# Causal attention with its heads side by side in 64-row tiles of float32r instead of three bfloat16 parts

## The chip, the cores and the metric

The kernel runs on one core of a Trainium2 chip. The time is device microseconds from launch to end, as the median of several runs. The core has five engines that run side by side: TensorE (matrix products, results into the eight banks of PSUM), VectorE, ScalarE, GpSimd and SyncE, whose queue SP starts transfers.

## What is computed

One layer on x of shape (2, 1024, 128), in float32: a modulated layer norm, causal attention with 16 heads of 8 numbers each, a residual, a second modulated norm and a mixture of eight experts (two for each token) with a shared one. Only the attention is changed. Cut to it:

```python
c_q = x @ W_dq
Q = (c_q @ W_uq).reshape(Bx, Sx, N_HEADS, D_K)
c_kv = x @ W_dkv
K = (c_kv @ W_uk).reshape(Bx, Sx, N_HEADS, D_K)
V = (c_kv @ W_uv).reshape(Bx, Sx, N_HEADS, D_K)
scores = jnp.einsum('bqhd,bkhd->bhqk', Q, K) / math.sqrt(D_K)
causal = jnp.tril(jnp.ones((Sx, Sx), dtype=bool))
scores = jnp.where(causal, scores, -jnp.inf)
attn = jax.nn.softmax(scores, axis=-1)
out = jnp.einsum('bhqk,bkhd->bqhd', attn, V).reshape(Bx, Sx, N_HEADS * D_K)
return out @ W_o
```

D_K is 8, Sx is 1024, and there are two batches.

## The kernel before

**Tasks.** The attention is cut into eight tasks, four heads of one batch each, and every task into two halves c of 512 queries. A task goes through two passes. In the first, `max_scores` (L1685) multiplies 128 queries by up to 512 keys for one head, and VectorE reduces each such unit to the row maximum (`max_unit`): a plain reduction (L1286) where all keys are allowed, and on the diagonal a combined add of a mask `later` and maximum (L1282). `maxima` (L1295) joins them, GpSimd splits the negated maxima into three bfloat16 parts (`split_max`, L674 to L677), TensorE turns them (`turn_max`, L1694), VectorE copies them (`neg_out`, L1303), and SP writes them as three more rows of the operands (`neg_rows`). In the second pass `score_unit` (L1716) multiplies 128 keys by up to 512 queries, so that the product comes with its maximum already subtracted. On the diagonal a product of the identity and the mask `after` is added (L1721). ScalarE takes the exponential (`exps`, L941). `weigh` (L1740) multiplies by the values, four heads at once in four 32-column tiles, in float32, and adds up in the bank `oacc[:, c]`; each of its products appears as two records in the trace. ScalarE copies that bank (`o_out`, L950), TensorE transposes it (`turn_out`, L1749), and VectorE divides (L1318, L1320).

**Operands.** A float32 number is the sum of three bfloat16 parts, made by `hi`, `residue`, `mid` and `low`. The parts go to memory and come back replicated, so that one contraction over 9 x 8 = 72 rows (CROSS) holds all products of parts; three rows of ones, or of the maxima, make 75. They lie in `S3`, a ring of three tasks, with a K side and a Q side. `load` brings one task: `load_k` three transfers, `load_q` three for each half.

**Order.** `attention_order` writes one list for all engines, and each engine walks through it in that order. The maxima run ahead of the scores: AHEAD units first, then some after every score unit (MAXES_AFTER), about a task of lead. The turn of the maxima stands SPLIT units behind their last one. A group (128 keys of one half) is weighed LAG score units after its last one; in all but the first and last task two groups are weighed together. BETWEEN and LATE put the late projections, the second norm and the router in between. FILLERS and FILL_AFTER are products without use early in the first task (`fill`).

**PSUM.** Three banks `sc` for scores, three `mx` for maxima and other units (`unit_banks` hands them out in turn), two `oacc`. `ring_free` makes TensorE wait until the engine that read a bank's last unit has freed it. So a score unit waits for the exponential three units back, and a unit of maxima for the reduction three units back.

After the attention come the routed experts: 39 tiles of 128 rows, products of 128 columns in float32 (L1873 and L1888) with the shared expert (L1829, L1840) in between.

## Time and profile before

| what | value |
|---|---|
| median of 3 runs | 430.55 us (429.49 to 431.08) |
| span of the profiled execution | 455.7 us; no other time of it is given |
| TensorE busy | 422.1 us (93%) |
| VectorE busy | 319.5 us (70%) |
| ScalarE busy | 268.1 us (59%) |
| GpSimd busy | 150.0 us (33%) |
| mean granted TensorE clock | 0.949 of full speed |
| first maxima of the attention | 24.1 us |
| first product of the routed experts | about 310 us |

The profile is of one execution. PE is TensorE's products, PEld its weight loads, DVE VectorE, ACT ScalarE, POOL GpSimd. Products are pipelined: one of 512 columns is shown 0.38 us long, while the next may begin 0.22 us after it began, so that distances between starts say more than lengths. The granted clock is 1.00 at 2.4 GHz and 0.50 at 1.2 GHz.

### The profile page before, as it was taken

Reading aid. Unit: us, or ns where it says so; the run is one execution under the profiler, and the core shown is the slowest. Engines: PE = TensorE matmul, PEld = TensorE weight load, DVE = VectorE, ACT = ScalarE, POOL = GpSimd, SP = SyncE. Lnnn points to the kernel's source line nnn. Section 1 sums busy time; section 2 is a strip of 40 time slices with the busy share of each in tenths; the row PEclk is TensorE's granted clock in tenths of the full one; section 3 lists DMA queues with packets and bytes.
Section 4 is the critical chain, followed back from the end, with each engine's and each line's share of the span. In section 5 each row is a group of like instructions: output and inputs, shape, how many; then the busy total and the mean of one; then the engine's idle time right before and its main releaser. Section 6 shows DMA issues by size and latency. Waiting matters only on the chain.

```text
span 455.7 us, 9455 instructions
## 1 busy us (share of the span) xinstructions
PE 422.1 (93%) x2963; PEld 242.9 (53%) x2963; DVE 319.5 (70%) x1185; ACT 268.1 (59%) x611; POOL 150.0 (33%) x244
## 2 busy tenths in 40 slices
PE   6989899999999999999999999999959779999984
PEld 3434423353443544454544434337747569999944
DVE  5768855788887987889797886355866435555646
ACT  3557344556666767675666576967446254555661
POOL 2246200026010020106556434231664743333520
PEclk9998855999999999999999999999989959999999
DMA  5245160034040210400400000960112223210126
GB/s 146 65 141 124 34 192 3 1 101 146 1 106 2 58 51 0 106 3 0 108 7 19 21 21 23 315 149 13 43 46 54 76 65 83 60 40 26 36 85 216
DMA packets 28796, 31.78 MB, mean 70 GB/s; under 512 B 4827, under 2 KB 23363, under 8 KB 28243
## 3 DMA queue, kind: packets, MB, share of 16 engines
q1 hardware_dynamic: 25959, 25.82, 20.0%
q0 software_dynamic: 2272, 4.67, 3.0%
q10 hardware_dynamic: 516, 0.69, 0.5%
q8 instruction: 24, 0.39, 0.4%
q14 instruction: 25, 0.20, 0.2%
HBM read 21.04 MB, written 9.85 MB: 68 GB/s over the span
## 4 chain that ended last, share of the span: by engine, by line
PE 71%; DVE 13%; issue 4%; DMA 4%; ACT 2%; another core or an unknown queue 2%; POOL 1%; SPq 1%; ACTq 0%; DVEq 0%; POOLq 0%
PE oacc L1740 15%; PE mx L1685 12%; PE sc L1716 12%; PE sc L1873 7%; PE oacc L1888 7%; DVE mxp L1286 4%; DVE masked L1282 3%; PE sc L1721 2%; PE mx L1840 2%; PE mx L1829 2%; PE mx L1749 1%; PE mx L1864 1%; PE sc L1829 1%; DMA S<-first_q_parts 1%
## 5 line engine op out<-in xcount | busy, mean ns | idle before, releaser
L941 ACT ACTIVATE pr<-sc 128x512 f32<-128x512 f32 (+1 forms) x295 | 156.2, 580 | 93.0 <-PE sc L1716 45.3
L1282 DVE CUSTOM_DVE_ANT_0 masked<-mx,later 128x128 f32<-128x128 f32 (+3 forms) x256 | 111.5, 485 | 19.4 <-PE mx L1685 18.7
L1685 PE MATMUL mx<-S 72*128 72x512 bf16 (+3 forms) x384 | 116.0, 344 | 6.4 <-DVE mxp L1282 2.2
L1716 PE MATMUL sc<-S 75*128 75x512 bf16 (+3 forms) x371 | 112.6, 339 | 0.7 <-ACT pr L941 0.6
L1286 DVE TENSOR_REDUCE mxp<-mx 128x1 f32<-128x512 f32 x128 | 82.9, 685 | 23.5 <-PE mx L1685 23.1
L1740 PE MATMUL oacc<-pr,vb 128*32 128x512 f32 (+3 forms) x768 | 77.9, 515 | 0.0
L1011 ACT ACTIVATE pr<-sc,bcur 128x128 f32<-128x128 f32 x156 | 44.5, 369 | 33.4 <-PE sc L1873 18.4
L1716 PEld LDWEIGHTS sc<-S 75*128 75x128 bf16 x371 | 35.3, 100 | 51.2 <-issue 28.6
L1685 PEld LDWEIGHTS mx<-S 72*128 72x128 bf16 x384 | 35.0, 101 | 48.0 <-DVE mxp L1282 19.2
L783 POOL DMA_INDIRECT token_results<-S,xrow x39 | 38.5, 988 | 61.7 <-DVE S L1432 59.6
L1888 PE MATMUL oacc<-vb,pr 128*128 128x128 f32 x312 | 42.8, 283 | 5.2 <-ACT pr L1011 5.2
L1888 PEld LDWEIGHTS oacc<-vb,pr 128*128 128x128 f32 x312 | 40.6, 199 | 12.8 <-ACT pr L1011 6.8
L1873 PE MATMUL sc<-xTg,vb 128*128 128x128 f32 x312 | 43.5, 284 | 3.5 <-ACT xTg L1003 1.2
L674 POOL CAST neg<-negm 128x16 bf16<-128x16 f32 x16 | 3.1, 196 | 129.2 <-DVE negm L1295 129.1
L1873 PEld LDWEIGHTS sc<-xTg,vb 128*128 128x128 f32 x312 | 39.5, 199 | 4.6 <-issue 3.2
L1721 PE MATMUL sc<-after,identb 128*128 128x128 bf16 (+2 forms) x171 | 41.9, 245 | 0.0
L777 POOL DMA_INDIRECT slot_rows<-parts,rowi x32 | 31.7, 989 | 29.9 <-PE sc L1716 12.1
L1740 PEld LDWEIGHTS oacc<-pr,vb 128*32 128x32 f32 x768 | 19.3, 111 | 35.7 <-issue 17.0
L1432 DVE TENSOR_TENSOR S<-oacc,be_sb 128x128 f32<-128x128 f32 x39 | 11.3, 290 | 31.5 <-PE oacc L1888 20.0
L1417 DVE COPY vb<-S 128x512 f32 x39 | 17.6, 451 | 19.9 <-issue 15.8
L1003 ACT ACTIVATE xTg<-mx 128x128 f32<-128x128 f32 x39 | 11.0, 283 | 22.2 <-PE mx L1864 15.6
L1282 DVE DVE_READ_ACCUMULATOR2_ANT mxp<- 128x1 f32 x256 | 21.0, 82 | 0.0
(294 smaller groups left out, 499.1 us busy)
## 6 DMA issues: line engine op xcount, KB each, us to landing
S<-k_parts SPq DMA_DIRECT2D x21, 192.0 KB
S<-q_parts SPq DMA_DIRECT2D x42, 96.0 KB
xrow<-slot_rows SPq DMA_DIRECT2D x39, 64.5 KB, 1.9
S<-in_we SPq DMA_DIRECT2D x1, 2048.0 KB, 9.7
S<-in_we SPq DMA_DIRECT2D x4, 512.0 KB, 10.4
parts<-token_results SPq DMA_DIRECT2D x4, 512.0 KB, 5.2
x_sb<-in_x SPq DMA_DIRECT2D x4, 256.0 KB, 3.9
out_y<-attn SPq DMA_DIRECT2D x4, 256.0 KB, 2.3
```

The lines of the kernel that those rows point to most:

```text
L777: pool.indirect_dma_start(xd, bass.IndirectOffsetOnAxis(ap=rowi[:, g, k, n:n + 1], axis=0), rowsk[:, g % 2, n, k, :], None).then_inc(sent[ ...
L783: pool.indirect_dma_start(yd, bass.IndirectOffsetOnAxis(ap=xrow[:, i % XR, C:C + 1].bitcast(I32), axis=0), yst[:, i % ROWS, :], None).then ...
L941: act.activation(pr[:, group % NBUF, h:h + n, at:at + w], src, ACT.Exp, scale=float(DK) ** -0.5).then_inc(s["exp_done"], 1)
L1011: ins = act.activation(hid[:, i % 2, P * f:P * f + P], sc[:, i % 2, P * f:P * f + P], ACT.Silu, bias=bcur[:, i % FREE, f:f + 1])
L1282: ins = dve.tensor_tensor_reduce(masked[:, d % 2, w * m:w * m + w], unit[a][:, w * m:w * m + w], later[:, HALF - w:HALF], 1.0, LOWEST, ALU ...
L1286: ins = dve.tensor_reduce(mxp[:, c, place, h:h + n, i - 4 * c], unit[a][:, 0:n * w].rearrange("p (h n) -> p h n", h=n), AX_X, ALU.max)
L1685: ins = pe.matmul(dst[:, w * m:w * m + w], S3[0:CROSS, r3, 1, q:q + P], S3[0:CROSS, r3, 0, kk:kk + w], start=(m == 0), stop=True, skip_gro ...
L1716: ins = pe.matmul(dst[:, w * m:w * m + w], S3[0:CROSS + 3, r3, 0, kk:kk + P], S3[0:CROSS + 3, r3, 1, q:q + w], start=(m == 0), stop=True, ...
L1721: ins = pe.matmul(dst[:, 0:n * w].rearrange("p (h n) -> p h n", h=n)[:, :, 0:P], identb[:, :], after[:, 0:n, :], start=False, stop=True, s ...
L1740: ins = pe.matmul(oacc[VW * h:VW * h + VW, c, at:HALF], vb[:, t % 2, j, h, :], pr[:, group % NBUF, h, at:HALF], start=(j == 0), stop=(j == ...
L1873: ins = pe.matmul(sc[:, i % 2, P * f:P * f + P], wcur[:, i % 2, P * f:P * f + P], xTg[:, i % 2, :], start=True, stop=True)
L1888: ins = pe.matmul(oacc[:, i % 2, 0:P], hid[:, i % 2, P * f:P * f + P], wcur[:, i % 2, FF + C * f:FF + C * f + C], start=(f == 0), stop=(f ...
```

## The change

- *Operands.* K and Q are split in two float32r parts, high and low, made by one ScalarE copy and one subtraction. The contraction has 2 x 2 x 8 = 32 rows, a row of ones or zeros (33 rows for the maxima) and two more for the two parts of the negated maximum (35 for the scores). `mid` and `residue` fall away.
- *Tiles.* Heads 0 and 1 of a task lie in partitions 0 to 63 (side 0), heads 2 and 3 in 64 to 127 (side 1). Each product uses one 64-row tile. A unit of maxima has both sides, in two neighbouring banks; a unit of scores has one side. There are 20 units of maxima for a task (38 before) and 40 of scores (38).
- *Masks.* Both passes add the mask by products over 64 rows, in two parts of 64 columns a head: `rows_of` picks rows, `stairs` holds the lowest number on one side of a diagonal. `later`, `masked` and the combined operation on VectorE are gone; `max_unit` is one reduction over two banks.
- *PSUM.* Four banks for maxima (two pairs), three for scores, one for the weighed sums, which both halves now share, so `weigh` waits at each first group for the copy of the half before.
- *Order.* AHEAD 12, one unit of maxima after each of the first 16 score units, then after every second one. SPLIT is 2. ScalarE copies the turned maxima (it was VectorE). The products without use are three after each of the first eleven units of maxima.
- *Transfers.* A task's operands come in 8 transfers (9 before), the maxima go back in two (one before).

```diff
+F32R = mybir.dt.float32r
...
-CROSS = 72
+PAIR = 2
+SIDE = 64
+PRODUCTS = 32
+ONES_AT = PRODUCTS + 1
 HALF = 512
-QW = HQ * HALF
+QW = PAIR * HALF
...
-            n = HALF // w if w < 384 else 1
+            n = 2 if w <= 256 else 1
             if c:
-                out += [(c, i, h, 1, 0, HALF, False, 0) for h in range(HQ)]
-            out += [(c, i, h, n, HALF * c, w, True, c) for h in range(0, HQ, n)]
+                out += [(c, i, h, 1, 0, HALF, False, 0) for h in range(PAIR)]
+            out += [(c, i, h, n, HALF * c, w, True, c) for h in range(0, PAIR, n)]
...
+            out += [(c, j, side, h, n, q0, w, P * j == q0) for h in range(0, PAIR, n) for side in range(2)]
...
-AHEAD = 20
-MAXES_AFTER = [2] * 4 + [3] * 4 + [2] * 2 + [1] * 5 + [2 if g % 4 == 0 else 1 for g in range(28)]
-FILL_AFTER = {9: 1, 10: 2}
-FILLERS = {(0, k): 2 if k < 3 else 1 for k in (0, 1, 2, 3, 4, 5, 7, 8, 10)}
-SPLIT = 5
+AHEAD = 12
+EXTRA_MAXES = 8
+FILLERS = 3
+SPLIT = 2
...
+          *[("turn", t, c) for t in range(8) for c in range(2)]}
...
+MX, SC, OA = (0, 1, 2, 3), (4, 5, 6), 7
...
+        if g % 2 == 0 or g < 2 * EXTRA_MAXES:
...
+        elif kind == "max":
+            banks = min((MX[0:2], MX[2:4]), key=lambda b: max(used[k] for k in b))
+        elif kind == "xturn":
+            banks = (SC[x[1] % 2],)
+        elif wide:
+            banks = (min((*SC, MX[0]) if kind == "score" else MX[1:4], key=lambda b: used[b]),)
+        elif kind == "score" or x in ON_ACT:
+            banks = (min(SC, key=lambda b: used[b]),)
...
-        sc = ctx.enter_context(nc.psum_tensor("sc", [P, RING, 512], F32))
-        mx = ctx.enter_context(nc.psum_tensor("mx", [P, RING, 512], F32))
-        oacc = ctx.enter_context(nc.psum_tensor("oacc", [P, 2, 512], F32))
+        mx = ctx.enter_context(nc.psum_tensor("mx", [P, 4, 512], F32))
+        sc = ctx.enter_context(nc.psum_tensor("sc", [P, 3, 512], F32))
+        oacc = ctx.enter_context(nc.psum_tensor("oacc", [P, 1, 512], F32))
...
-        after = sb("after", [P, HQ, P], BF16)
-        later = sb("later", [P, HALF], F32)
-        masked = sb("masked", [P, 2, HALF], F32)
+        warmb = sb("warmb", [P, HALF], BF16)
+        stairs = sb("stairs", [P, 2, SIDE], BF16)
+        rows_of = sb("rows_of", [P, 2, 2, P], BF16)
...
-        parts = sb("parts", [P, 2, 3, NT * P], BF16)
+        parts = sb("parts", [P, 2, 2, NT * P], F32)
...
+        with nc.sbuf_tensor("operands", [P, 3, 2, 2 * QW], F32) as S3:
+            S3r = S3[:, :, :, :].bitcast(F32R)
...
-                for a in range(3):
-                    sp.dma_start(S3[24 * a:24 * a + 24, r3, 0, :].rearrange("r (h n) -> r h n", h=HQ)[:, :, cols],
-                                 src).then_inc(sem, 16)
+                for side in range(2):
+                    src = kd[b, u, :, :, PAIR * side:PAIR * side + PAIR, cols].rearrange("d a h n -> (d a) h n")
+                    for a in range(2):
+                        at = SIDE * side + 2 * DK * a
+                        sp.dma_start(S3[at:at + 2 * DK, r3, 0, :].rearrange("r (h n) -> r h n", h=PAIR)[:, :, cols],
+                                     src).then_inc(sem, 16)
...
+            chained(pool.memset(stairs[:, :, :], LOWEST))
+            chained(pool.memset(rows_of[:, :, :, :], 0.0))
+            for side in range(2):
+                half, first = slice(SIDE * side, SIDE * side + SIDE), slice(SIDE * side, SIDE * side + 1)
+                chained(pool.affine_select(out=stairs[half, 0], in_=stairs[half, 0], compare_op=ALU.is_ge, fill=0.0,
+                                           base=0, pattern=[[1, SIDE]], channel_multiplier=-1))
...
-                chained(pool.tensor_copy(neg3[:, c, 0, :], negm[:, c, :]))
-                chained(pool.tensor_tensor(negr[:, c, :], negm[:, c, :], neg3[:, c, 0, :], ALU.subtract))
-                chained(pool.tensor_copy(neg3[:, c, 1, :], negr[:, c, :]))
-                pool.tensor_tensor(neg3[:, c, 2, :], negr[:, c, :], neg3[:, c, 1, :],
-                                   ALU.subtract).then_inc(s["neg3_ready"], 1)
+                chained(pool.tensor_copy(neg2[:, c, :, 0, :].bitcast(F32R), sides(negm[:, c, :])))
+                pool.tensor_tensor(neg2[:, c, :, 1, :].bitcast(F32R), sides(negm[:, c, :]), neg2[:, c, :, 0, :],
+                                   ALU.subtract).then_inc(s["neg2_ready"], 1)
...
+            def neg_out(t, c, a):
+
+                act.wait_ge(s["aux_ready"], a + 1)
+                if t >= 1:
+                    act.wait_ge(s["negrow"], 32 * (2 * t + c - 1))
+                act.activation(negT[:, c, :], unit[a][0:2 * HQ * 4, 0:P], ACT.Copy).then_inc(s["act_free"], 1)
...
+                own = mx[:, HELD["max", t, k][0]:HELD["max", t, k][0] + 2, 0:n * w]
                 dve.wait_ge(s["aux_ready"], a + 1)
-                if diagonal:
-
-                    d = DIAGONAL.index((t, k))
-                    if d >= 2:
-                        dve.wait_ge(*freed(("max", *DIAGONAL[d - 2])))
-                    for m in range(n):
-                        ins = dve.tensor_tensor_reduce(
-                            masked[:, d % 2, w * m:w * m + w], unit[a][:, w * m:w * m + w], later[:, HALF - w:HALF],
-                            1.0, LOWEST, ALU.add, ALU.max, mxp[:, c, place, h + m, i - 4 * c:i - 4 * c + 1])
-                else:
-                    ins = dve.tensor_reduce(mxp[:, c, place, h:h + n, i - 4 * c], unit[a][:, 0:n * w].rearrange(
-                        "p (h n) -> p h n", h=n), AX_X, ALU.max)
-                ins.then_inc(s["aux_free"], 1)
+                dve.tensor_reduce(sides(mxp[:, c, place, :, i - 4 * c])[:, :, h:h + n],
+                                  own.rearrange("p s (m w) -> p s m w", m=n), AX_X, ALU.max).then_inc(s["aux_free"], 1)
 
             def maxima(t, c):
...
+            def operand(r3, side, rows, kq, at, n):
+
+                return S3r[SIDE * side:SIDE * side + rows, r3, kq, at:at + n]
...
-                dst = unit[a]
+                    pe.wait_ge(s[f"first_in{c}"], 16 * 6)
                 for m in range(n):
-                    q = QW * (i // 4) + HALF * (h0 + m) + P * (i % 4)
-                    kk = S * (h0 + m) + k0
-                    ins = pe.matmul(dst[:, w * m:w * m + w], S3[0:CROSS, r3, 1, q:q + P],
-                                    S3[0:CROSS, r3, 0, kk:kk + w], start=(m == 0), stop=True,
-                                    skip_group_check=(m > 0))
+                    q = QW * (i // 4) + HALF * (h + m) + P * (i % 4)
+                    kk = S * (h + m) + k0
+                    for side in (1, 0):
+                        dst = bank[HELD["max", t, k][side]]
+                        ins = pe.matmul(dst[:, w * m:w * m + w], operand(r3, side, ONES_AT, 1, q, P),
+                                        operand(r3, side, ONES_AT, 0, kk, w), start=(m == 0), stop=True,
+                                        skip_group_check=(m > 0))
+                if diagonal:
+                    for part in range(2):
+                        for side in (1, 0):
+                            dst = bank[HELD["max", t, k][side]][:, 0:n * w].rearrange("p (m w) -> p m w", m=n)
+                            at = w - P + SIDE * part
+                            own = slice(SIDE * side, SIDE * side + SIDE)
+                            ins = pe.matmul(dst[:, :, at:at + SIDE], rows_of[own, 0, part, :], stairs[own, 0:1, :].broadcast_to([SIDE, n, SIDE]),
+                                            start=False, stop=True, skip_group_check=True)
...
+                dst = bank[HELD["score", t, k][0]]
                 for m in range(n):
-                    kk = S * (h0 + m) + P * j
-                    q = QW * c + HALF * (h0 + m) + q0 - HALF * c
-                    ins = pe.matmul(dst[:, w * m:w * m + w], S3[0:CROSS + 3, r3, 0, kk:kk + P],
-                                    S3[0:CROSS + 3, r3, 1, q:q + w], start=(m == 0), stop=True,
+                    kk = S * (h + m) + P * j
+                    q = QW * c + HALF * (h + m) + q0 - HALF * c
+                    ins = pe.matmul(dst[:, w * m:w * m + w], operand(r3, side, ONES_AT + 2, 0, kk, P),
+                                    operand(r3, side, ONES_AT + 2, 1, q, w), start=(m == 0), stop=True,
                                     skip_group_check=(m > 0))
                 if diagonal:
-
-                    ins = pe.matmul(dst[:, 0:n * w].rearrange("p (h n) -> p h n", h=n)[:, :, 0:P], identb[:, :],
-                                    after[:, 0:n, :], start=False, stop=True, skip_group_check=True)
+                    own = slice(SIDE * side, SIDE * side + SIDE)
+                    for part in range(2):
+                        ins = pe.matmul(dst[:, 0:n * w].rearrange("p (m w) -> p m w", m=n)[:, :, SIDE * part:SIDE * part + SIDE],
+                                        rows_of[own, 1, part, :], stairs[own, 1:2, :].broadcast_to([SIDE, n, SIDE]), start=False, stop=True,
+                                        skip_group_check=True)
                 ins.then_inc(s["score_ready"], 1)
...
-                if j == 0 and t >= 1:
-                    pe.wait_ge(s["o_done"], 2 * t + c - 1)
-                elif j == 0 and c == 1:
-                    pe.wait_ge(*freed(("val", 3, 0)))
-                if k == 0 and t in BACK:
-                    pe.wait_ge(*freed(BACK[t]))
+                if j == 0 and 2 * t + c:
+                    pe.wait_ge(s["o_done"], 2 * t + c)
                 for h in range(HQ):
-                    ins = pe.matmul(oacc[VW * h:VW * h + VW, c, at:HALF], vb[:, t % 2, j, h, :],
+                    ins = pe.matmul(oacc[VW * h:VW * h + VW, 0, at:HALF], vb[:, t % 2, j, h, :],
...
-                    pe.matmul(dst, identb[:, :], parts[:, 0, 0, 0:HALF], start=True, stop=True)
+                    pe.matmul(bank[OA], identb[0:SIDE, :], warmb[0:SIDE, :], start=True, stop=True)
```

The helpers `freed`, `bank_free` and `unit_banks` are otherwise adapted to the new names: a bank's next user waits for the reader of its last one.

## Rows read from the trace of the kernel before

**Rows 1.** The page: span, busy time of each engine, granted TensorE clock in 40 slices.

```profile
span 455.7 us, 9455 instructions
...
PE 422.1 (93%) x2963; PEld 242.9 (53%) x2963; DVE 319.5 (70%) x1185; ACT 268.1 (59%) x611; POOL 150.0 (33%) x244
...
PEclk9998855999999999999999999999989959999999
```

**Rows 2.** The page: the chain that ended last, by engine and by line.

```profile
PE 71%; DVE 13%; issue 4%; DMA 4%; ACT 2%; another core or an unknown queue 2%; POOL 1%; SPq 1%; ACTq 0%; DVEq 0%; POOLq 0%
PE oacc L1740 15%; PE mx L1685 12%; PE sc L1716 12%; PE sc L1873 7%; PE oacc L1888 7%; DVE mxp L1286 4%; DVE masked L1282 3%; PE sc L1721 2%; PE mx L1840 2%; PE mx L1829 2%; PE mx L1749 1%; PE mx L1864 1%; PE sc L1829 1%; DMA S<-first_q_parts 1%
```

**Rows 3.** The chain in order of time: start us, length us, what.

```profile
105.90 1.89 DVE mxp L1286 x3
110.10 1.85 PE oacc L1740 x16
...
121.73 1.64 PE oacc L1740 x16
125.07 0.79 PE oacc L1740 x16
...
135.44 1.89 DVE mxp L1286 x3
...
165.86 1.89 DVE mxp L1286 x3
...
284.25 0.06 PE sc L1721
...
292.41 1.00 PE oacc L1740 x8
...
378.11 0.89 PE sc L1873 x8
```

**Rows 4.** Windows: busy us of each engine (count), granted clock, DMA share, GB/s.

```profile
52.00:56.00 4.00, 2.96 (x15) 1.46 (x16) 3.52 (x21) 0.88 (x3) 0.97 (x4) 0.77 0.04 9
56.00:80.00 24.00, 24.00 (x90) 6.96 (x92) 13.58 (x41) 9.74 (x17) 0.83 (x4) 0.50 0.33 98
130.00:160.00 30.00, 29.70 (x232) 13.25 (x230) 25.38 (x90) 20.95 (x41) 2.19 (x10) 1.00 0.17 44
```

**Rows 5.** Timeline of TensorE in one steady task: start us, length us, instructions.

```profile
133.21 0.40 PE L1685 MATMUL mx<-S 72*128 72x128 bf16 x4
...
135.02 0.38 PE L1685 MATMUL mx<-S 72*128 72x512 bf16 x1
135.24 0.38 PE L1716 MATMUL sc<-S 75*128 75x512 bf16 x1
...
136.36 0.66 PE L1749 MATMUL mx<-ident,osb 128*128 128x128 f32 x4
```

**Rows 6.** Timeline of VectorE in the same task.

```profile
139.10 1.88 DVE L1286 TENSOR_REDUCE mxp<-mx 128x1 f32<-128x512 f32 x3
...
143.15 0.55 DVE L1282 CUSTOM_DVE_ANT_0 masked<-mx,later 128x384 f32<-128x384 f32 x1
...
143.62 0.55 DVE L1282 CUSTOM_DVE_ANT_0 masked<-mx,later 128x384 f32<-128x384 f32 x1
```

**Rows 7.** Timeline of ScalarE in the same task.

```profile
136.19 3.64 ACT L941 ACTIVATE pr<-sc 128x512 f32<-128x512 f32 x7
```

**Rows 8.** The page: costliest groups, busy us, mean ns, idle us before and its releaser.

```profile
L941 ACT ACTIVATE pr<-sc 128x512 f32<-128x512 f32 (+1 forms) x295 | 156.2, 580 | 93.0 <-PE sc L1716 45.3
...
L1716 PEld LDWEIGHTS sc<-S 75*128 75x128 bf16 x371 | 35.3, 100 | 51.2 <-issue 28.6
...
L1873 PEld LDWEIGHTS sc<-xTg,vb 128*128 128x128 f32 x312 | 39.5, 199 | 4.6 <-issue 3.2
...
L1003 ACT ACTIVATE xTg<-mx 128x128 f32<-128x128 f32 x39 | 11.0, 283 | 22.2 <-PE mx L1864 15.6
```

385 lines of the change are left out of this document (166 added, 219 removed).

## The prediction

> **What bounds it now.** I read the page first: TensorE is busy 93% of the span, and the row of granted clock is full except in a few slices [rows 1]. The chain that ended last is 71% TensorE, led by the weighing of values (L1740) and the two kinds of score products (L1685, L1716); the reductions on VectorE hold 6.5% of it [rows 2]. So the attention is a TensorE stage with VectorE close behind. The windows say how close: in 30 us of steady attention TensorE is busy 29.7, VectorE 25.4, ScalarE 21.0 [rows 4].
>
> The period of a task (four heads of one batch) is read in the chain from a piece that recurs: 105.90, 135.44, 165.86, so 29.5 and 30.4 us; I use 30.0 [rows 3]. There are eight tasks. Their maxima run a task ahead, so the first stretch has many maxima and the last task none.
>
> **TensorE's sum for one task now.** Products: 4,608 columns a head for the maxima and as many for the scores, times four heads, 36,864 columns. Starts of neighbouring 512-column products lie 0.22 us apart (135.02, 135.24) [rows 5]; 72 blocks' worth make 15.7. Masks: 32 blocks of 128 columns at 0.06 us, 1.9 [rows 3]. Weighing: six pairs of groups, 1.64 + 0.79 + 1.85 + 1.85 + 1.64 + 0.79 = 8.6 [rows 3]. Two sets of output transposes, 0.6 each, and two turns of maxima: 1.6. Together 27.8; the other 2.2 are gaps and waits.
>
> **The change on TensorE.** (a) *Products.* A head contracts 33 or 35 rows of float32r instead of 72 or 75 of bfloat16, in a 64-row tile; two heads, one in each half of the rows, write to different banks. The order makes the neighbours alternate: score of side 0, maxima of side 1 and side 0, score of side 1. Columns and count (96 a task) stay. Nothing in this trace shows a row tile or a float32r product, so I bound both. Tiles do overlap on this array: eight weighing records of 512 columns in four column tiles take 1.0 us (292.41) [rows 3], where a float32 record alone takes two cycles a column, 0.11 us for 128 (378.11, eight in 0.89) [rows 3], thus 0.43 for 512 and 3.4 for eight. Below, then: one cycle a column, sides fully overlapped, 7.9 us. There each instruction has only 0.11 us for a 512-column product, and its weights must be loaded in that time. The bfloat16 weight load is 100 ns and streams at 0.055 us each (four products of 128 columns in 0.40, the last's latency taken off) [rows 5, 8]; a float32 load is 199 ns and streams at 0.11 [rows 3, 8]. If that holds here, 96 x 0.111 = 10.7. I take the middle, 9.3. Above, two cycles a column or no overlap give 15.7, and that is a rival below.
>
> The Trainium skill (TensorE: Matmul & The Clock Gate, Weight-path perf modes) says that fast weight load needs a dtype other than FP32. The trace agrees in direction, 199 ns against 100; by the page the sum would be the 10.7 rather than 9.3.
>
> (b) *Masks.* TensorE now masks the maxima as well. A task has 24 diagonal score units and 12 diagonal maxima units of two sides, each with two 64-column products: 96 instead of 22 instructions, for half the rows. At 0.06 each 5.8; if 64 columns or a pair of sides halve that, 2.9; I take 4.3, which is 2.4 more than now. The Trainium skill (TensorEngine Tiling (Array Packing), Instruction Overhead) gives some 60 cycles to any small matmul; by it 64 columns gain next to nothing over 60, and 96 would be an estimated 2.4 to 4.8 us. No row here shows a 64-column product.
>
> (c) *The rest stays*: weighing, transposes, turns, gaps. The alternation of tile shapes before and after each weighing is there now too. Sum: 9.3 + 4.3 + 8.6 + 1.6 + 2.2 = 26.0, bounds 23.2 and 28.9 (7.9 + 2.9, and 10.7 + 5.8).
>
> **What is late next.** *VectorE.* Now the reductions of 512 columns start 0.60 us apart (three in 1.88, the last 0.69 long) and the masked ones of 384 0.48 [rows 6], that is columns / 0.96 GHz plus 0.06 to 0.08: 16 x 0.60 + 8 x (0.21 + 0.35 + 0.48 + 0.61) = 22.8 a task. After: 20 reductions over two banks, the same 18,432 columns / 0.96 = 19.2, plus 20 x 0.065 = 20.5. The other 2.6 us (25.4 - 22.8) lose two copies of the turned maxima, 0.4. So 22.7 a task: the accumulator reads are gone, but VectorE gains only 2.7 of 25.4. *ScalarE.* Exponentials of 512 columns run at 0.51 us (seven in 3.64) [rows 7], 427 ns of columns and 80 fixed; two more units and two copies of about 0.28 (that of 128 columns, L1003) [rows 8] make 21.0 + 0.7 = 21.7. Both lie under 26.0, but three engines within 4 us, with two pairs of banks for the maxima (before, three single ones) and a weighing of 1.85 us blocking TensorE at a time, can't all be fed. Below 24.5 I don't believe it. Taken: 26.2.
>
> *The single output bank.* The next half's weighing waits for ScalarE's copy. It lies four to eight units later, 2 to 4 us against a 0.6 us exponential and a 0.6 us copy; with that cover gone each of 16 handovers would cost up to 0.6. I take 2 us in all. *The turn* comes two units after its last maximum, about 2.5 us, and waits for 0.19 on VectorE and two GpSimd steps (four before) of 0.2; it costs at most some tenths, and queued behind it are the products that both other engines wait for. It is in the 0.2 between 26.0 and 26.2. *Transfers.* A task's operands came in 9 DMAs, 72 rows of 4,096 two-byte numbers a side; now they come in 8, 64 rows of 2,048 four-byte ones, with a task of slack (share 0.17 in the window) [rows 4]. The maxima rows go back in two DMAs instead of one, 40 units before the scores need them. SP's queue before the first stores gets three more, at a time when it waits for the parts. *The start.* A middle part vanishes (two 0.6 us copies, two or three slow GpSimd subtractions), but four instead of three loads follow for each half; I leave it at nothing. GpSimd builds stairs and row patches with some 20 short chained steps, hidden behind the same loads.
>
> **The sum.** Six ordinary tasks save 30.0 - 26.2 = 3.8 each: 22.8. The first, filled by VectorE, saves 2.3 (22.8 - 20.5). The last has no maxima, ScalarE and dependent steps set it: 1 taken. Minus 2 for the bank: 24 us. The profiled execution is known by its span, 455.7, which is 25.1 over the median of 430.55; no other time of it is given. Some of the excess is in places that the change doesn't touch: the 24 us at half clock (12 lost) [rows 4] and waits in the experts. So I take the difference at face value: 430.5 - 24 = 407. Its bounds: 1.1 (28.9) to 5.5 (24.5) in each of six tasks, 7 to 36 in all with the rest, so 395 to 423.
>
> **Rivals.** *1. The products don't get cheaper* (slower). One cause: float32r needs two cycles a column, like each float32 record; or one: the row tiles run one after the other. Either gives 15.7 + 4.3 for 17.6, +2.4 a task (0.9 to 4.0), and eight tasks 19: 450 (437 to 462). It decides as soon as products plus masks exceed 17.6. For it: every one-pass float32 row, the transposes of 128 columns (four in 0.66) [rows 5], starts 0.11 apart, two cycles a column. Against: those may be held by their own weight loads. 19%. Both causes at once, 31.4: 18 us a task, about 575; 4%.
>
> *2. The clock.* At 52 to 56 TensorE was busy 2.96 of 4 us and the clock fell to half; it stayed there until 80 though the engine was busy all 24.0 of the 24 us [rows 4]. After the change TensorE waits more. A task at half clock is 50 us instead of 26, so one task's work in that state takes the whole gain, and two give 455 (430 to 500). Against: 100 to 310 ran at full clock with the present mix, and 26 of 26.2 us is no idle engine. 14%.
>
> *3. The gain is eaten by waits* among VectorE, ScalarE and the pairs of banks: 29 to 30 us a task, 425 to 433. For it: ScalarE already waits 93 us ahead of its exponentials [rows 8]. 11%.
>
> **Numbers.** The forecast has 52%; its time is 407, its own range 395 to 423. About 0.5% (2.2 us) can be told from no change. Faster: 52 + 5 of rival 3 + 1 of rival 2, 58%. Same: 7%. Slower: 35%. The range 395 to 456 holds most of the forecast, rival 3 and the lower part of rivals 1 and 2, some 80%.
>
> **What will show it.** The L1685 and L1716 groups: starts of two sides nearly together and a 512-column pair each 0.22 us (right), or 0.43 (rival 1). The period of a task 26 us; VectorE's reductions of 1,024 columns 1.13 us apart and its busy share near 87%; masks 0.03 to 0.06 each; the clock row full between 100 and 280. Wrong if the weight loads of float32r are longer than 0.11, if small masks drain the array, or if half-clock stretches return.

## The result and the profile after

The changed kernel takes 534.91 us (median of 4 runs, 531.37 to 554.35), the kernel before 430.81 beside it: a ratio of 1.237, 95% interval 1.228 to 1.247. The forecast was 407, its range ended at 456. Executions of one program differ in the clock that they are granted, so the ratios here are of the faster ones alone, and the profile of the kernel before (455.7 us, mean granted clock 0.949, 44 us at half) is of a slower one than its timed runs near 430 us (0.995, by which I estimate some 4 us at half). The page of the changed kernel, in the parts that answer to [rows 1, 2, 8]:

```profile
span 529.9 us, 10032 instructions
PE 496.1 (94%) x3573; PEld 304.0 (57%) x3573; DVE 306.3 (58%) x688; ACT 266.9 (50%) x635; POOL 141.4 (27%) x225
...
PEclk9955555555987857767998798789569999999999
...
PE 77%; DVE 8%; DMA 4%; ACT 4%; issue 4%; POOL 2%; SPq 1%; DVEq 0%; POOLq 0%; ACTq 0%
...
L1261 DVE TENSOR_REDUCE mxp<-mx 128x2 f32<-128x1024 f32 (+3 forms) x160 | 176.4, 1118 | 122.2 <-PE mx L1658 60.9
L932 ACT ACTIVATE pr<-sc 128x512 f32<-128x512 f32 (+2 forms) x310 | 154.7, 560 | 147.1 <-PE sc L1697 101.4
L1691 PE MATMUL sc<-operands 35*128 35x512 f32 (+3 forms) x372 | 130.1, 490 | 1.4 <-ACT pr L932 0.8
L1658 PE MATMUL mx<-operands 33*128 33x512 f32 (+3 forms) x384 | 121.3, 505 | 5.8 <-DMA operands<-k_parts 4.0
```

The reader is to see the clock row first. Before, it was full but for a few slices [rows 1]; now eight slices in a row are at 5, and most of the attention after them changes between the two levels. Summed over the granted clock's stretches, 212 us of 530 are at half clock (1.2 GHz), against 44 of 456 in the profile before. The share of busy TensorE rose from 93 to 94% while VectorE and ScalarE fell: TensorE isn't idle, it is slow. The windows of the changed kernel (us; busy time and count of PE, PEld, DVE, ACT, POOL; granted clock; DMA) say it in one line each:

```profile
28.00:40.00 12.00, 12.00 (x53) 5.56 (x51) 5.85 (x7) 2.94 (x4) 0.00 (x0) 0.50 0.44 119
76.00:88.00 12.00, 11.79 (x82) 7.00 (x82) 7.11 (x8) 4.05 (x9) 0.64 (x3) 0.50 0.64 129
112.00:124.00 12.00, 12.00 (x101) 7.36 (x98) 5.23 (x6) 5.24 (x12) 0.42 (x2) 0.50 0.01 3
136.00:148.00 12.00, 10.80 (x91) 5.48 (x89) 8.39 (x11) 8.92 (x19) 9.08 (x8) 1.00 0.33 117
256.00:268.00 12.00, 10.41 (x77) 6.08 (x74) 7.91 (x14) 8.46 (x16) 0.00 (x0) 1.00 0.01 3
```

In 28 to 40 and 112 to 124 TensorE was busy all 12 of 12 us and stayed at half clock; the half-clock stretch runs from 27.8 to 133.6 without a break. The Trainium skill (TensorE: Matmul & The Clock Gate, Part 1: The HAM clock gate) says that the clock follows how busy the array has been and that a busy one gets 2.4 GHz. These windows don't bear that out, if busy means the profile's busy time; the runs below say what has to be added.

Where the clock is full, the new form is as quick as I had hoped. The timeline of TensorE in the changed kernel (start, length, both in us):

```profile
258.72 0.51 PE L1658 MATMUL mx<-operands 33*128 33x512 f32 x2
259.05 0.41 PE L1691 MATMUL sc<-operands 35*128 35x512 f32 x2
259.29 0.40 PE L1658 MATMUL mx<-operands 33*128 33x512 f32 x2
259.53 0.44 PE L1691 MATMUL sc<-operands 35*128 35x512 f32 x1
260.63 1.13 PE L1761 MATMUL mx<-wog,hT 128*128 128x128 f32 x8 [0.67 <-DVE mxp L1261]
```

Each row but the fourth and the last is a pair, one product in each half of the rows (PE L1658 is the maxima, L1691 the scores). Pairs start 0.24 us apart at best (259.05, 259.29). 512 columns in 0.24 us at 2.4 GHz are about one cycle a column for both halves at once, so float32r doesn't need two and the halves overlap; rival 1 falls. The last row shows the other side of it: a wait for VectorE.

### The profile page after: what moved, and what is told of

The parts are those of the page before. It is cut to its first block, busy times and chain, and to the rows that moved or that the text cites. A ratio compares the mean times of both kernels' runs of the same rounds, so it can differ in the third digit from the quotient of the medians.

```text
span 529.9 us, 10032 instructions
## 1 busy us (share of the span) xinstructions
PE 496.1 (94%) x3573; PEld 304.0 (57%) x3573; DVE 306.3 (58%) x688; ACT 266.9 (50%) x635; POOL 141.4 (27%) x225
## 4 chain that ended last, share of the span: by engine, by line
PE 77%; DVE 8%; DMA 4%; ACT 4%; issue 4%; POOL 2%; SPq 1%; DVEq 0%; POOLq 0%; ACTq 0%
PE oacc L1713 20%; PE sc L1691 14%; PE mx L1658 11%; PE sc L1846 5%; PE sc L1697 3%; PE mx L1863 2%; PE oacc L1863 2%; DVE mxp L1261 2%; PE mx L1667 2%; PE mx L1722 2%; PE oacc L1870 2%; PE mx L1813 2%; PE sc L1570 2%; ACT pr L932 1%; POOL slot_rows L783 1%
## 5 line engine op out<-in xcount | busy, mean ns | idle before, releaser
L1261 DVE TENSOR_REDUCE mxp<-mx 128x2 f32<-128x1024 f32 (+3 forms) x160 | 176.4, 1118 | 122.2 <-PE mx L1658 60.9
L932 ACT ACTIVATE pr<-sc 128x512 f32<-128x512 f32 (+2 forms) x310 | 154.7, 560 | 147.1 <-PE sc L1697 101.4
L1691 PE MATMUL sc<-operands 35*128 35x512 f32 (+3 forms) x372 | 130.1, 490 | 1.4 <-ACT pr L932 0.8
L1658 PE MATMUL mx<-operands 33*128 33x512 f32 (+3 forms) x384 | 121.3, 505 | 5.8 <-DMA operands<-k_parts 4.0
L1713 PE MATMUL oacc<-pr,vb 128*32 128x512 f32 (+3 forms) x768 | 109.4, 691 | 0.1
L1691 PEld LDWEIGHTS sc<-operands 35*128 35x128 f32 x372 | 65.5, 229 | 67.3 <-issue 45.1
L1658 PEld LDWEIGHTS mx<-operands 33*128 33x128 f32 x384 | 63.1, 238 | 20.2 <-issue 12.9
L1009 ACT ACTIVATE pr<-sc,bcur 128x128 f32<-128x128 f32 x156 | 44.6, 368 | 27.8 <-PE sc L1846 27.7
L789 POOL DMA_INDIRECT token_results<-late,xrow x39 | 38.6, 989 | 57.5 <-DVE late L1399 54.1
L1697 PE MATMUL sc<-stairs,rows_of 64*128 64x64 bf16 (+1 forms) x372 | 47.1, 233 | 0.0
L1667 PE MATMUL mx<-stairs,rows_of 64*128 64x64 bf16 (+1 forms) x384 | 43.2, 237 | 0.0
L1384 DVE COPY vb<-weights 128x512 f32 x39 | 17.7, 453 | 21.7 <-issue 11.5
```

Of the source, the lines that this page charges most:

```text
L789: pool.indirect_dma_start(yd, bass.IndirectOffsetOnAxis(ap=xrow[:, i % XR, C:C + 1].bitcast(I32), axis=0), yst[:, i % ROWS, :], None).then ...
L932: act.activation(pr[:, group % NBUF, h:h + n, at:at + w], src, ACT.Exp, scale=float(DK) ** -0.5).then_inc(s["exp_done"], 1)
L1009: ins = act.activation(hid[:, i % 2, P * f:P * f + P], sc[:, i % 2, P * f:P * f + P], ACT.Silu, bias=bcur[:, i % FREE, f:f + 1])
L1261: dve.tensor_reduce(sides(mxp[:, c, place, :, i - 4 * c])[:, :, h:h + n], own.rearrange("p s (m w) -> p s m w", m=n), AX_X, ALU.max).then_ ...
L1658: ins = pe.matmul(dst[:, w * m:w * m + w], operand(r3, side, ONES_AT, 1, q, P), operand(r3, side, ONES_AT, 0, kk, w), start=(m == 0), stop ...
L1667: ins = pe.matmul(dst[:, :, at:at + SIDE], rows_of[own, 0, part, :], stairs[own, 0:1, :].broadcast_to([SIDE, n, SIDE]), start=False, stop= ...
```

## The experiments

All runs were set beside runs of the kernel before on the same chip (430.8 to 433.2 us). Where the third column has times, they are the lowest and the highest run, and no ratio is on record. Half-clock time is that of the profiled execution, without the stretch at its very end, at most 3.4 us. The period is the distance between ScalarE's copies of a task's first output (`osb<-oacc`) from the second task to the fifth, divided by three.

| kernel | median us | ratio (95%), or range of the runs | us at half clock | period us |
|---|---|---|---|---|
| before | 430.81 | | 44 | 29.8 |
| changed | 534.91 | 1.237 (1.228 to 1.247) | 212 | 39.1 |
| e1 rows filled up to 64 | 476.94 | 1.102 (1.094 to 1.110) | 65 | 31.1 |
| e2 before, on 24 and 27 rows | 598.71 | 1.384 (1.375 to 1.392) | 345 | 51.6 |
| e3 bfloat16 | 477.49 | 1.108 (1.099 to 1.116) | 106 | 30.7 |
| e4 fills, 64 rows | 516.6 | 501.88 to 523.56 us | 113 | 35.2 |
| e5 = e1 + single weighs | 476.88 | 1.109 (1.100 to 1.118) | 58 | 31.6 |
| e6 = e1 + start on 128 rows | 465.69 | 1.074 (1.064 to 1.085) | 24 | 31.1 |
| e7 = e4 with 128 rows | 636.87 | 1.474 (1.464 to 1.485) | 256 | 46.4 |
| e8 joined | 465.79 | 1.081 (1.073 to 1.089) | 21 | 31.6 |
| e9 = e6, half exponentials | 458.4 | 1.058 (1.048 to 1.069) | 21 | 29.8 |
| e10 = e6, half reductions | 458.54 | 1.062 (1.052 to 1.073) | 14 | 30.6 |
| e11 = e6, no masks | 457.12 | 1.057 (1.047 to 1.067) | 31 | 29.7 |
| e12 = e9 + e10 | 444.23 | 1.030 (1.022 to 1.037) | 10 | 28.1 |
| e13 = e6, another queue | 461.54 | 456.94 to 464.90 us | 10 | 31.1 |
| e14 = e12, no masks | 428.93 | 0.992 (0.988 to 0.997) | 24 | 26.2 |
| e15 = e1 + fills on 128 rows | 466.08 | 1.079 (1.075 to 1.083) | 27 | 31.1 |
| e16 = e6, later weighing | 464.83 | 1.074 (1.068 to 1.081) | 34 | 31.3 |
| e18 changed, fills on 128 rows | 533.69 | 523.20 to 546.56 us | 188 | 39.1 |
| e19 = e14 in bfloat16 | 412.81 | 0.958 (0.952 to 0.963) | 10 | 24.4 |

### What takes the clock away

**e1**, the changed kernel with the contraction filled up with zero rows to 62 (maxima) and 64 (scores) a half:

```diff
-ONES_AT = PRODUCTS + 1
+ONES_AT = SIDE - 2
...
-                    at = SIDE * side + PRODUCTS
+                    at = SIDE * side + ONES_AT - 1
...
+            chained(pool.memset(S3[:, :, :, :], 0.0))
```

> The changed kernel with contractions of 62 and 64 rows instead of 33 and 35 (the rows added hold zeros in both operands; the rows of the negated maxima move to 62 and 63; GpSimd writes zeros once at the start, some 11 us beside the first loads). Columns, count, order and waits stay. If the clock falls because few rows of the array work in the products, the clock rises well above 0.80 and the time falls towards 450 us. If it falls because TensorE streams a smaller share of the time (share theory), nothing moves: 530 to 545 us, clock 0.76 to 0.81.

**e2**, the kernel before with only the first of the three parts of Q against the three parts of K (the products and transfers of the other parts of Q are left out), so 24 and 27 rows instead of 72 and 75; same tiles, same columns, same order:

```diff
-CROSS = 72
+CROSS = 24
...
-                            q0[c].rearrange("a d h n -> (a d) (h n)").unsqueeze(1).broadcast_to([3 * DK, 3, QW])
+                            q0[c, 0].rearrange("d h n -> d (h n)").unsqueeze(1).broadcast_to([DK, 3, QW])
...
-                for a in range(3):
+                for a in range(1):
```

> The kernel before with only the high part of Q against the three parts of K: contractions of 24 and 27 rows instead of 72 and 75 (the products with the middle and low parts of Q are left out, and their transfers). Columns, count, order and waits stay. Rows theory: the clock falls as in the changed kernel, and the time rises to 480 or more. Share theory: the clock stays as in the kernel before and the time is 425 to 433 us.

**e3**, the changed kernel with its operands read as bfloat16 (the low bits are dropped), the rows as changed:

```diff
-                return S3r[SIDE * side:SIDE * side + rows, r3, kq, at:at + n]
+                return S3b[SIDE * side:SIDE * side + rows, r3, kq, 2 * at + 1:2 * (at + n):2]
```

> The changed kernel with the same operands read as bfloat16 (the upper two bytes of each float32 number, so the lowest bits of the operands are left out); rows, tiles, columns and order stay. If the number format (its weight loads or its slower streaming) costs the time, it falls by 30 us or more and products of 512 columns start closer together. Share theory: the products take no more than before and the engine waits even more, so the clock is no higher and the time within 15 us of 532.

**e4**, the changed kernel with a product of zeros over 64 rows and 512 columns behind score units (205 products over zeros in all):

```diff
+                    if open_half:
+                        pe.matmul(bank[OA], warmb[0:SIDE, 0:P], warmb[0:SIDE, :], start=False, stop=True,
+                                  skip_group_check=True)
```

> The changed kernel with one more product without use of 512 columns behind each score unit while a half's weighed sums are open (about 30 a task; zeros added to the output bank, 0.22 us each at full clock, some 7 us a task). If TensorE's own work were the bound at whatever clock, the time rises by 50 us or more. Share theory: the engine streams more of the time, the clock rises above 0.9, and the time falls to 450 to 490 us although there is more work.

The clock rows of e1, e2, e3 and e4, each from its own page:

```profile
PEclk9985558599999999999989999988999999999998
```
```profile
PEclk9995555566765557575598686656555999999998
```
```profile
PEclk9965556798998899899897858998999999999998
```
```profile
PEclk9965555698996599899798799999999999999999
```

e1 adds nothing but zeros in rows that the 64-row tile already spans: TensorE gets no instruction and no column more. It takes 58 us off, and the stretches at half clock fall from 212 to 65 us. The gain would be larger but for the zeros themselves. They were expected "beside the first loads", and they are not: GpSimd writes them for 10.3 us at the very start, and the first maxima come at 34.1 us instead of 26.8. GpSimd's row of e1, then the row of the first maxima in the chains of e1 and of the changed kernel:

```profile
3.44 10.34 POOL L621 MEMSET operands<- 128x12288 f32 x1
```
```profile
34.11 0.69 PE mx L1659 x4
```
```profile
26.81 0.44 PE mx L1658 x4
```

These 7.3 us are in every kernel built on e1 (e5, e6 and e8 to e16, and e19).

e2 goes the other way: the old kernel, whose profile shows full clock from 81.5 to 334 us, loses it when its score and maxima products use a third of the rows, and takes 168 us more. Two of its windows:

```profile
52.00:64.00 12.00, 11.64 (x48) 3.55 (x48) 7.01 (x34) 2.28 (x4) 1.17 (x5) 0.50 0.14 37
64.00:76.00 12.00, 12.00 (x47) 3.07 (x46) 6.16 (x16) 4.83 (x9) 0.84 (x4) 0.50 0.32 96
```

So the granted clock depends on how many rows the products use; the time that the engine is busy doesn't tell it alone. e3 takes 57 us off and shows that this isn't all: at the changed kernel's 33 and 35 rows bfloat16 has 106 us of half clock where float32r has 212. e4 makes TensorE do more and its median is 18 us lower: its four runs, 501.88 to 523.56, all lie under the changed kernel's, 531.37 to 554.35. Neither of its two expected ranges was met.

**e7**, e4 with the added products over 128 rows:

```diff
-                        pe.matmul(bank[OA], warmb[0:SIDE, 0:P], warmb[0:SIDE, :], start=False, stop=True,
+                        pe.matmul(bank[OA], warmb[:, 0:P], warmb[:, :], start=False, stop=True,
                                   skip_group_check=True)
```

> The kernel of e4 (zero products put between the score units) with these products over 128 rows instead of 64, of the same number of columns, so of the same time. Theory A (the clock follows the rows that products use as well as the time they take): clock over 0.93 in the profile, the whole 465 to 500 us. Theory B (only TensorE's busy time counts): the same clock and time as e4, 505 to 530 us.

Neither came: 636.87 us. Part of it is plain: in e7's timeline at full clock a product over all rows runs beside neither half. It and the products before and behind it start 0.32 to 0.33 us apart (220.07, 220.39, 220.72, 221.04), and even in the stretch at full clock (177 to 259 us) a task took 43 us. But the clock was no better than the changed kernel's, 256 us at half in a span of 640, the same 40% of it, and "more rows, more clock" doesn't say why. Perhaps the heads' products, now thinner in time, count for more than products of zeros; that wasn't tried, and stays open.

The opening has two sorts of fills. Ahead of the first maxima stand 18 in a row, over 128 rows in both kernels (`warm`). Behind each of the first eleven units of maxima stand three, 33 in all (`fill`); these have 64 rows in the changed kernel. **e6** is e1 with 32 instead of 18 of the first sort and 128 rows for the second; **e15** has the rows alone; **e18** has the rows alone in the changed kernel itself:

```diff
-            warm(18)
+            warm(32)
...
-                    pe.matmul(bank[OA], identb[0:SIDE, :], warmb[0:SIDE, :], start=True, stop=True)
+                    pe.matmul(bank[OA], identb[:, :], warmb[:, :], start=True, stop=True)
```

> The kernel of e1 with the products that keep TensorE busy before the first maxima read over 128 rows instead of 64, and 32 instead of 18 of them. Theory A: the first long stretch at half clock (31.8 to 69.4 us, and 79.6 to 96.7) comes from the pause and the few rows ahead of it; then it goes or is much shorter, and the whole is 450 to 460 us. Theory B: the stretch comes from the first two tasks' own products, whatever is before them: within 1% of e1's 477 us.

> The kernel of e1 with the opening's filling products over 128 rows instead of 64, and 18 before the first maxima as in e1. Theory A (rows in use keep the clock): most of e6's gain, 464 to 470 us and no stretch of half clock over 20 us. Theory B (it was the 14 more products, which bridge the wait for the operands): 474 to 480 us, as e1.

> The changed kernel itself, with one edit: the opening's filling products over 128 rows instead of 64 (36 of them, as before in number and columns). Theory A (rows in use decide, wherever they come from): the first stretch at half clock, 27.8 to 133.6 us, starts later or is much shorter, but later stretches stay, since the heads' own products use 33 and 35 rows a half: 495 to 520 us. Theory B (the opening does not matter, the heads' products decide): within 1.5% of 534.9.

e6 lies between its two theories in time, and its longest stretch at half clock is 14 us where e1 has 38. e15 gives all of e6's gain (466.08 and 465.69, from 476.94), as its theory A has it: the rows of the 33 fills did it, not the 14 more ahead of them. Nothing but these rows differs between e1 and e15, while e2 has fewer transfers too and e1 its late start. By themselves, in e18, they don't decide: the median of 533.69 is the changed kernel's, though the two quickest of the four runs, 523.20 and 527.49, lie under all of the changed kernel's. Half clock begins in earnest at 49.6 instead of 27.8 us and holds to 124.7, and then it comes and goes as in the changed kernel, whose heads' products still use 33 and 35 rows. That the rows of the fills were halved (in the kernel before they are 128) was part of the change too.

### What a task costs at full clock

e1 and e6 have their clock nearly everywhere and still need 31.1 us a task, 4.9 more than I forecast and 1.3 more than before.

**e5**, e1 with every group weighed by itself (`pair = 1`), **e8**, e5 with e6's start and the last product of a task in the score banks, **e16**, e6 with `LAG` 5 instead of 3:

> The kernel of e1 (rows filled up to 62 and 64 with zeros) with every group weighed by itself, not two groups interleaved in one unit. Theory A: at full clock a task takes 30.7 to 31.8 us because the unit that weighs two groups side by side holds TensorE for 1.85 us in which nothing for VectorE and ScalarE is made; single weighs lose the overlap (16 tasks of 8 groups) but feed the other two engines evenly. By it a task at full clock falls to some 27 to 28 us and the whole to 425 to 445 us. Theory B: the overlap of the two tiles is worth more than even feeding; single weighs add TensorE time (about 0.9 us a group pair) and the whole is 490 to 520 us.

> Joined: rows filled up as in e1, single weighs as in e5, the longer start over 128 rows as in e6, and the last product of a task in the banks of the scores, so that no two units of maxima follow each other on one pair of banks. If the three causes are the clock at the start, the uneven feeding and the in-order waits, it comes under the kernel before: 395 to 420 us. If the paired form's own waits between three engines remain at 30 us a task, it is 440 to 460 us, and no version of this layout beats the kernel before.

> The kernel of e6 with each weighing two score units later (5 units behind its group's last score, not 3). Theory A (TensorE waits at the weighing for the last exponential, and ScalarE then idles for the 1.9 us of the weighing): the period falls by 0.5 to 1.5 us a task, the whole to 455 to 462. Theory B (ScalarE's idle time comes from the three banks of scores, whatever the lag): within 0.5% of 465.7.

None of the three shortened the period (31.6, 31.6, 31.3). The idle time that a pair's weighing leaves on ScalarE is there, but splitting or moving the weighing gains nothing. Theory A of e5 and e16 was wrong (e5 lies outside theory B too, e16 agrees with its theory B), and e8's 465.79 lies outside both of its ranges.

**e9** halves the columns of the exponentials in tasks 2 to 8, **e10** those of the reductions, **e12** both, **e11** leaves out the mask products, **e14** is e12 without masks. What each leaves out or changes is said in its expectation.

```diff
+                z = w if t == 0 else w // 2
-                own.rearrange("p s (m w) -> p s m w", m=n), AX_X, ...
+                own.rearrange("p s (m w) -> p s m w", m=n)[:, :, :, 0:z], AX_X, ...
...
-                act.activation(pr[:, group % NBUF, h:h + n, at:at + w], src, ACT.Exp,
+                act.activation(pr[:, group % NBUF, h:h + n, at:at + z], src, ACT.Exp,
...
-                if diagonal:
+                if False:
```

> The kernel of e6 in which the exponentials of tasks 2 to 8 cover only half of each score unit's columns (the other half of the weights keeps older values, and the scale is changed so that all stay finite). ScalarE's 512-column step falls from 0.51 to about 0.25 us; TensorE's and VectorE's work stays. Theory A: at full clock the 30.7 to 31.8 us of a task are set by ScalarE between two weighings (eight units of 0.44 to 0.51, then 1.9 us in which it waits); then the period falls by over 2 us, to 28 or less, and the whole to 445 or less. Theory B: TensorE's own instructions fill the period: it stays over 30 and the whole within 1% of e6's 465.7.

> The kernel of e6 in which the reductions of the maxima in tasks 2 to 8 cover only half of the columns (so the maxima are of half the keys, and the scale is changed so that the exponentials stay finite). VectorE's 1.12 us for two banks falls to about 0.6. Theory A (the two pairs of banks for maxima, held by VectorE for 1.1 us each, stop TensorE's queue): the period falls from 31 to 28 to 29 us, the whole to 445 to 455. Theory B (VectorE is off the path): within 1% of e6's 465.7.

> The kernel of e6 without the 96 mask products a task (scores and maxima are then of all keys, not of the earlier ones alone). My sum gave them 4.3 us a task, 2.9 to 5.8. Theory A (TensorE's instructions fill the period): it falls by about as much, to 26 to 28 us, the whole 430 to 445 if the clock stays. Theory B (ScalarE and VectorE set it between the weighings): it stays over 29.5 us; with less work on TensorE the clock may even fall and the whole be slower.

> The cuts of e9 and e10 together (half of the exponentials' and half of the reductions' columns in tasks 2 to 8), TensorE's work unchanged. What is left is TensorE's own time in this order. If my sum of 26.0 us a task (products 9.3, masks 4.3, weighing 8.6, 1.6, gaps 2.2) is right, the period at full clock is 25 to 27 us and the whole 410 to 430; if the products and masks cost more than I gave them (18.5 us instead of 13.6, as the steady task of e6 leaves after weighing and turns), it stays at 30 to 31 and the whole at 455 to 466.

> The kernel of e12 (half of the exponentials' and of the reductions' columns in tasks 2 to 8) without the mask products as well. What is left of a task on TensorE is products, weighing, transposes. By my sum that is 9.3 + 8.6 + 1.6 + 2.2 = 21.7 us. Theory A (the two row tiles overlap as I took it): 21.5 to 24 us a task at full clock. Theory B (three score banks that come free one by one let only a score and a maxima unit, or nothing, run side by side, so that products cost 4 us more): 25 to 27 us a task, the whole 425 to 440.

From 31.1 us the period falls by 1.3 with half the exponentials, by 0.4 with half the reductions, by 3.0 with both, by 1.4 without masks, and by 4.9 with all three. Against the expectations: e9 and e10 lie between their theories, e11 keeps to its theory B (over 29.5), e12's 28.1 lies between its two cases, and e14's 26.2 and 428.93 are its theory B. Waits among the three engines hold 3 us and more. The masks cost 1.9 us where least else waits (28.1 to 26.2), 0.02 us each; I gave them 4.3. The Trainium skill (TensorEngine Tiling (Array Packing), Instruction Overhead) gave an estimated 2.4 at its lower end: nearer than mine, and still above what the runs show. But what is left for products, weighing and transposes is 26.2, where my terms make 21.7. TensorE's timeline in e14, between two weighings at full clock:

```profile
142.20 1.92 PE L1716 MATMUL oacc<-pr,vb 128*32 128x512 f32 x16
144.06 0.50 PE L1694 MATMUL sc<-operands 64*128 64x512 f32 x2
144.39 0.40 PE L1661 MATMUL mx<-operands 62*128 62x512 f32 x2
144.63 0.89 PE L1694 MATMUL sc<-operands 64*128 64x512 f32 x2
145.03 0.73 PE L1661 MATMUL mx<-operands 62*128 62x512 f32 x2
145.36 0.70 PE L1694 MATMUL sc<-operands 64*128 64x512 f32 x2
145.64 0.60 PE L1661 MATMUL mx<-operands 62*128 62x384 f32 x2
145.99 0.78 PE L1694 MATMUL sc<-operands 64*128 64x512 f32 x2
146.54 0.44 PE L1661 MATMUL mx<-operands 62*128 62x384 f32 x2
146.91 1.92 PE L1716 MATMUL oacc<-pr,vb 128*32 128x512 f32 x16
```

Eight pairs in 2.85 us: 0.36 a pair. I had taken 9.3 us for 48 pairs of 384 columns, 0.19 a pair, which is some 0.26 for 512. **e19** asks whether the weight loads stand in it: e14 with the operands read as bfloat16, over the same rows.

> The kernel of e14 (half of the columns on ScalarE and VectorE, no masks) with the heads' operands read as bfloat16 instead of float32r, over the same 62 and 64 rows; the low bits are dropped. Theory A (the float32r weight loads are not hidden behind the products, 0.11 us a pair of halves): the 16 products between two weighings take 2.0 to 2.3 us instead of 2.85, a task 23 to 24.5 us instead of 26.2. Theory B (the score banks pace them): 2.7 us and over, a task 25.7 us or more.

The weight loads of e14 and e19 in 110 to 167 us (count, busy us, mean ns), then e19's timeline of the block like the one above:

```profile
L1694 PEld LDWEIGHTS sc<-operands 64*128 64x128 f32 x101 | 14.5, 184 | 11.7 <-issue 6.8 <-ACT pr L934 3.4
```
```profile
L1695 PEld LDWEIGHTS sc<-operands 64*128 64x128 bf16 x115 | 7.9, 94 | 19.6 <-issue 8.3 <-ACT pr L935 7.9
```
```profile
135.20 0.40 PE L1695 MATMUL sc<-operands 64*128 64x512 bf16 x2
135.44 0.39 PE L1662 MATMUL mx<-operands 62*128 62x512 bf16 x2
135.67 0.80 PE L1695 MATMUL sc<-operands 64*128 64x512 bf16 x2
136.07 0.62 PE L1662 MATMUL mx<-operands 62*128 62x512 bf16 x2
136.35 0.67 PE L1695 MATMUL sc<-operands 64*128 64x512 bf16 x2
136.63 0.56 PE L1662 MATMUL mx<-operands 62*128 62x384 bf16 x2
136.94 0.67 PE L1695 MATMUL sc<-operands 64*128 64x512 bf16 x2
137.49 0.34 PE L1662 MATMUL mx<-operands 62*128 62x384 bf16 x2
137.76 1.93 PE L1717 MATMUL oacc<-pr,vb 128*32 128x512 f32 x16
```

The load's record halves, the block falls to 2.56 us and the task to 24.4, by 1.8. The block lies between the two theories, the task in theory A's range. The first three rows start 0.24 and 0.23 apart, while three score banks are empty. Then the step is 0.40, to 136.07, and from there every score product starts 0.06 us after one of ScalarE's exponentials ended (136.02, 136.29, 136.57, 136.89 and 137.16): it waits for its bank, one bank after the other. Loads hold 1.8 us of the 4.5 that the sum lacked; the banks probably hold most of the rest, which is argued from these rows and not tried by itself.

### The first task

**e13**, e6 with the first maxima rows sent by ScalarE's queue:

```diff
             store_parts(0)
-            neg_rows(0, 0)
...
+                        if (t, k) == (0, 0):
+                            act.wait_ge(*freed(("turn", 0, 0)))
+                            for side in range(2):
+                                act.dma_start(S3[...], negT[...]).then_inc(s["negrow"], 16)
```

> The kernel of e6, in which the maxima rows of the first half task go to the scores' operands by ScalarE's queue and not by SyncE's, where they stand behind the stores of all parts. Theory A (they land at 57.3 us, 9.4 us after their issue, because they wait behind those stores): they land after 2 to 4 us, the first score starts near 51 instead of 57.5, and the whole falls by 4 to 7 us, to 459 to 462. Theory B (VectorE's maxima or other work would have held the first scores nearly as long): the first score comes earlier, the end does not, within 0.5% of 465.7.

The chain of e6 in order of time, ahead of its first score:

```profile
46.27 0.24 ACT negT L949
...
46.53 1.39 SPq L530
...
47.96 9.36 DMA operands<-negT
...
57.45 0.47 PE sc L1692
```

In e13 this transfer is off the chain, but the first exponential starts at 57.0 instead of 58.0, so something else stood close behind. The median falls by 4.2 us, into theory A's range, but not by its mechanism (a first score near 51): the runs overlap (456.94 to 464.90, against 459.95 to 466.97), and the profile has 10 us of half clock against 24. No more than 1 us is shown to be the queue's.

The first exponential starts at 60.1 in the changed kernel and at 40.3 in the one before. In the changed kernel the transfer isn't in the chain: from 26.8 us to the first score it is TensorE alone, at half clock from 27.8 on. In e18, where the fills have 128 rows, the first exponential comes at 50.8, and the chain is the transfer's again (9.07 us, to 49.73); in the kernel before it was issued at 37.0, some 3 us before the first exponential. And in e15, which differs from e18 by e1's rows of zeros, it comes at 58.1: the 7.3 us of the zeros. So of the 19.8 us some 9 are the clock of the opening and some 10.5 the change's own. The groups of TensorE in 20 to 60 us of the changed kernel and in 20 to 40.3 of the one before:

```profile
L1870 PE MATMUL oacc<-warmb,identb 64*128 64x512 bf16 x33 | 15.7, 611 | 0.0
L1658 PE MATMUL mx<-operands 33*128 33x512 f32 (+3 forms) x35 | 14.5, 623 | 4.0 <-DMA operands<-k_parts 4.0
```
```profile
L1685 PE MATMUL mx<-S 72*128 72x512 bf16 (+3 forms) x32 | 8.2, 336 | 2.4 <-DMA S<-first_q_parts 2.2
L1895 PE MATMUL sc<-parts,identb 128*128 128x512 bf16 x12 | 4.1, 379 | 0.0
```

The change puts three fills behind each of eleven units of maxima, 33 against 12, and they take 15.7 us, nearly all at half clock, against 4.1. In the same stretch VectorE, of whose reductions the first score's maxima consist, waits for TensorE:

```profile
L1261 DVE TENSOR_REDUCE mxp<-mx 128x2 f32<-128x1024 f32 (+3 forms) x12 | 13.1, 1093 | 23.2 <-PE mx L1667 15.7 <-PE mx L1658 7.5
```

That the number of fills costs time in the changed kernel is read from these rows; a version with fewer wasn't run.

## Why the prediction was wrong

**The clock decided, and I weighed it against the wrong thing.** The sum has no term for the clock. The step that failed is in rival 2, which was to justify that: "26 of 26.2 us is no idle engine", against "100 to 310 ran at full clock with the present mix". Both sentences look at busy time. The mix changed in another way, 33 and 35 rows a product instead of 72 and 75, and fills over 64 rows, and e1, e2 and e15 show that rows count. Rival 2 had the rest right: a task at half clock takes about 50 us (52.3 between the first and the second copy, 86.9 and 139.2 us, of which all but 5.6 us were at half clock). Its chance was 14% and its size two tasks; it was 212 us. From the changed kernel to e6, which differ in rows in use, in 14 fills and in the zeros of 7.3 us, it is 69 of the 128 us by which I was out.

I had the warning in hand: at 56 to 80 us of the kernel before TensorE was busy all 24 us and remained at half clock [rows 4]. I read it as a consequence of the idle time before it, and didn't ask what else could hold it there.

**The products** were right in kind (one cycle a column, halves overlap, rival 1 refuted at 19 and 4%) and too cheap in size: "the middle, 9.3" between 7.9 and 10.7. e14 takes 26.2 for what my terms make 21.7, e19 puts 1.8 of that to the float32r loads, which I knew (the 10.7 was from them) and averaged away. That a score product waits for its bank, and may then run with nothing beside it in the other half, was in no term. The rule on fast weight load that I had set beside it (the Trainium skill, TensorE: Matmul & The Clock Gate, Weight-path perf modes) points the right way: e19 agrees with 94 ns against 184.

**The masks**, 4.3, were too dear by 2.4, which hid half of the former. **The weighing**, 8.6, is 9.0 (six pairs of 16 records, the group's 18.0 us for two tasks).

**What is late next.** "Taken: 26.2" left 0.2 for waits in three engines within 4 us. They are 3 us or more (e12). Rival 3, 29 to 30 us a task, was nearly the truth at full clock: 31.1. Of 4.9 us over the forecast, 3.0 are these waits and some 2 the net of products and masks; over six tasks that is 29 us.

**The start**, "I leave it at nothing", cost 19.8 us before the first exponential in the changed kernel, 10.5 of them still there when the fills have 128 rows (e18) and 17.7 in e6, where 7.3 are e1's zeros. The transfer of the maxima rows, which I had put "40 units before the scores need them", is needed at once in the first task and takes 9.1 us in e18 and 9.4 in e6, and the 33 fills, which the diff names, had no term at all. The single output bank, to which I gave 2 us, shows nowhere: the weighings of e6 have 0.1 us of idle time ahead of them in the whole span.

Together: 69 us of clock, 29 of period, 18 of start, 116 of 128. An estimate of the rest: e6 itself has 24 us at half clock where the timed runs of the kernel before have some 4, and half of the difference, 10 us, is lost. Of the 18, 7 are the experiment's zeros and not the change, so the change's start is nearer 11 and its clock, with both corrections, nearer 86.

No version that I ran beats the kernel before and computes the same. e13, with the lowest median, takes 461.54 us, 31 more. Its first exponential comes 17 us later (7 of them by the zeros), its period is 1.3 us longer in six tasks, which makes 8, and some 3 are its 10 us at half clock.

## What to carry to other kernels

Before a contraction is made shorter, compare the rows in use and not only the columns: a full array of products over fewer rows can lose the clock, and filling the tile with zero rows, which costs TensorE no instruction, can bring most of it back. Write the zeros where nothing waits for the engine that writes them; here they held the first maxima back by 7.3 us. A saving on one engine counts only up to what the next two need in the same order with the banks there are; cut their work in halves, one by one and together, to find out how much that is. And give each instruction that a diff adds to the opening a term of its own, useless products too, because nothing hides it there.

## What the hardware showed unexpectedly

- Granted clock 0.50 for 106 us on end (27.8 to 133.6), while TensorE was busy 10.95 to 12.00 us of every 12, at 33 and 35 rows a half. 24 and 27 rows in the old form: 345 us at half clock instead of 44. Zero rows in the same tiles: 65 instead of 212.
- The number format counts too: 106 us at half clock as bfloat16, 212 as float32r, at the same rows. A product of zeros over 128 rows behind the score units did not lift the clock (256 us of 640, the changed kernel 212 of 530), one over 64 rows did (113 of 500). Neither is explained here.
- Two float32r products of 512 columns in the two halves of the rows start together, and pairs follow each other after 0.24 us; a product over all 128 rows among them starts 0.32 us after one and before another; a float32r load of 64 rows by 128 takes 184 ns, a bfloat16 one 94.
- A mask product over 64 rows, of 64 or twice 64 columns, adds 0.02 us on average (96 of them, 1.9 us, e12 to e14).
